# Building the routing lists per expert group by group in a graph-and-experts kernel

## What is computed

```python
x = x + einsum(segment_sum(layernorm(x)[src] * edge_weight[:, None], dst), W) + b
xf = layernorm(x)
H = gelu(xf @ W1 + b1)                        # 256 -> 1024
probs = softmax(H @ Wg + bg)                  # 8 experts
assign = argmax(probs)
y = H @ Wd[e] + bd[e]                         # for the assigned e only: 1024 -> 256
x = x + probs[assign] * y
```

## Time and profile before

| | us |
|---|---|
| median of 3 runs | 2820.1 |
| lowest and highest run | 2818.66, 2824.56 |
| span of the profiled execution | 2820.7 |
| PE busy, DVE busy, ACT busy, POOL busy in it | 2418.9, 988.5, 444.4, 1847.0 |

### The profile page before, as it was taken

How to read it: one execution, slowest core, us unless ns; L and a number is a source line. 1 busy time by engine, 2 the same in 40 slices (tenths; PEclk the granted TensorE clock), 3 DMA queues, 4 the chain that set the end, 5 groups by cost and what they waited for, 6 DMA issues and landing times.

```text
span 2820.7 us, 40486 instructions
## 1 busy us (share of the span) xinstructions
PE 2418.9 (86%) x11774; PEld 1410.7 (50%) x11775; DVE 988.5 (35%) x2788; ACT 444.4 (16%) x847; POOL 1847.0 (65%) x1988
## 2 busy tenths in 40 slices
PE   0468998998889889899899899898998968999998
PEld 0133444444444444444444444444444447888887
DVE  8421333333333323333233333233332463333332
ACT  7000011000111000110001101011100102443442
POOL 0677777777777777777777777777777103555553
PEclk9988999999999999999999999999999989999999
DMA  9433444444444444444444444444444254555553
GB/s 390 151 111 112 149 146 137 120 140 149 147 149 125 126 149 148 147 141 120 138 145 148 147 118 132 148 150 148 143 121 133 90 177 129 184 183 176 183 184 126
DMA packets 153599, 420.32 MB, mean 149 GB/s; under 512 B 33320, under 2 KB 67499, under 8 KB 150880
## 3 DMA queue, kind: packets, MB, share of 16 engines
q0 software_dynamic: 100032, 300.27, 35.8%
q1 hardware_dynamic: 53536, 119.73, 11.4%
HBM read 328.02 MB, written 92.82 MB: 149 GB/s over the span
## 4 chain that ended last, share of the span: by engine, by line
POOL 46%; PE 31%; issue 17%; DVE 2%; DMA 2%; DVEq 0%; ACT 0%; SPq 0%; POOLq 0%; ACTq 0%
POOL big L391 46%; PE psA L519 4%; PE psH L560 4%; PE psA L641 3%; PE psG L641 3%; PE psH L641 3%; PE psE L641 3%; PE psR L503 2%; PE psE L509 1%; DMA src_i<-in_srcT 1%; PE psA L581 1%; PE psA L538 1%; PE psH L631 1%; PE psE L631 1%; PE psA L631 1%
## 5 line engine op out<-in xcount | busy, mean ns | idle before, releaser
L391 POOL DMA_INDIRECT big<-xn_table,src_i x1664 | 1615.2, 971 | 581.5 <-issue 580.0
L519 PE MATMUL psA<-w,ident 128*128 128x512 f32 x1664 | 735.5, 595 | 0.0
L519 PEld LDWEIGHTS psA<-w,ident 128*128 128x128 f32 x1664 | 308.5, 190 | 347.9 <-issue 347.9
L503 PE MATMUL psR<-big,sel_narrow 128*32 128x256 f32 x3328 | 258.7, 464 | 220.9 <-DMA big<-xn_table,src_i 158.6
L454 ACT ACTIVATE hidT<-psH,b 128x512 f32<-128x512 f32 x200 | 137.4, 687 | 1651.6 <-PE psH L560 1651.6
L560 PE MATMUL psH<-xn2T,w 128*128 128x512 f32 x800 | 351.4, 592 | 0.7 <-ACT xn2T L449 0.7
L503 PEld LDWEIGHTS psR<-big,sel_narrow 128*32 128x32 f32 x3328 | 116.0, 128 | 369.0 <-issue 333.5
L877 DVE COPY parts<-psR 128x512 f32<-128x512 f32 x104 | 71.8, 690 | 563.3 <-PE psR L503 562.9
L560 PEld LDWEIGHTS psH<-xn2T,w 128*128 128x128 f32 x800 | 152.1, 190 | 181.5 <-issue 179.2
L509 PE MATMUL psE<-w,ident 128*128 128x512 f32 x416 | 224.2, 664 | 0.0
L405 POOL COPY stage<-rel_f 128x1 int32 (+1 forms) x105 | 19.2, 183 | 250.9 <-DVEq L1065 144.3
(11 more groups left out here) (203 smaller groups left out, 2343.4 us busy)
## 6 DMA issues: line engine op xcount, KB each, us to landing
row_table<-rows SPq DMA_DIRECT2D x25, 2064.0 KB, 7.9
big<-xn_table,src_i POOLq DMA_INDIRECT x1664
big<-in_x SPq DMA_DIRECT2D x10, 1280.0 KB, 17.4
xn_table<-big SPq DMA_DIRECT2D x10, 1280.0 KB, 12.8
big<-in_x SPq DMA_DIRECT2D x25, 512.0 KB
row_table<-big SPq DMA_DIRECT2D x25, 512.0 KB, 3.9
big<-in_Wd SPq DMA_DIRECT2D x8, 1024.0 KB, 11.9
hidT<-in_dstT SPq DMA_DIRECT2D x2, 840.0 KB, 30.3
```

Source lines behind the costliest of these rows:

```text
L391: nc.gpsimd.indirect_dma_start(out=xring[:, h * STEP_TILES + j, :], out_offset=None, in_=xn_dram[:, :], in_offset=bass.IndirectOffsetOnAxi ...
L503: mm = nc.tensor.matmul(psQ[j * LANES:(j + 1) * LANES, o * C:(o + 1) * C], sel_narrow[:, t, :], xring[:, t, :], start=(odd == 0), stop=(od ...
L519: nc.tensor.matmul(psA[0][:, :], ident[:, :], w1[:, 0, 0:512], start=True, stop=True)
```

## The change

It builds the order of nodes by expert while the groups are worked on, in place of behind the loop.

- `choose`, at the end of `second_part(f)`, turns group f's logits into a one-hot of its nodes' experts (`chosen`), on DVE.
- `rank_list`, at the start of `hidden(f)` on PE, ranks the choices of group f-1 within their experts: 8 matmuls. `rank_choices` on DVE, between normalisation and evictions, makes a column one-hot and four slot one-hots of them. `extend_list`, on PE behind the hidden matmuls, multiplies these: 4 matmuls. `add_to_lists` on DVE adds the result to eight lists (128 x 104 each) at places that it loads into registers, and counts.
- Behind the loop, groups 23 and 24 are still to be listed. Then DVE pads the counts, copies the eight lists one after another into `merged` at register places, each over the padding of the one before, and works out owners and node numbers as it did.
- All of the routing from L978 to L1041, L609 to L624 and the buffer `logits` go.
- SP loads `Wd` and `bd` when the last edge step and the last take of sums are through, ahead of the store of group 24's rows.
- DVE's loop has one place for a group's first part (group 0's too), `second_part` behind it under its own If, and the wide variant as a loop of two tiles with two one-hot buffers in place of four.

The core of the diff:

```diff
@@ SP
-            store_rows(NF - 1)
-            sp.wait_ge(s_main, 1)
+            sp.wait_ge(s_edge_mm, TILES + MM0)
+            sp.wait_ge(s_ffn, (NF - 1) * FFN_LINKS + 2)
             for e in range(E):
                 sp.dma_start(wd[:, e * HC:(e + 1) * HC, :],
                              Wd[e].rearrange("(c p) o -> p c o", p=P)).then_inc(s_wd, 16)
             sp.dma_start(bd_bc, bd.rearrange("e c -> (e c)").partition_broadcast(P)).then_inc(s_bd, 16)
+            store_rows(NF - 1)
@@ PE
+            def rank_list(b):
+                pe.wait_ge(s_chosen, b + 1)
+                oh = chosen[:, :, :].rearrange("p q e -> p (q e)")
+                at, total = list_rank, list_total
+                nc.tensor.matmul(psE[0][:, at], upper[:, :], oh, start=True, stop=False)
+                for d in range(1, QB):
+                    nc.tensor.matmul(psE[0][:, at.start + d * E:at.stop], ones[:, :], oh[:, 0:(QB - d) * E],
+                                     start=False, stop=(d == QB - 1))
+                for q in range(QB):
+                    mm = nc.tensor.matmul(psE[0][:, total], ones[:, :], oh[:, q * E:(q + 1) * E],
+                                          start=(q == 0), stop=(q == QB - 1))
+                mm.then_inc(s_rank, 1)
+
+            def extend_list(b):
+                pe.wait_ge(s_rank_oh, b + 1)
+                for q in range(QB):
+                    mm = nc.tensor.matmul(psE[0][:, list_new], slot_oh[:, q, :], col_oh[:, q, :],
+                                          start=(q == 0), stop=(q == QB - 1))
+                mm.then_inc(s_list, 1)
             def hidden(f, following=None):
+                rank_list(f)
                 pe.wait_ge(s_xtc, f * KC + KC)
...
                     mm.then_inc(s_h, 1)
+                extend_list(f)
                 pe.wait_ge(s_gelu, f * HC + HC)
...
                 pe.wait_ge(s_gc, f + 1)
+                pe.wait_ge(s_listed, f + 1)
@@ DVE
+            def rank_choices(tie, b):
+                dve.wait_ge(s_chosen, b + 1)
+                dve.wait_ge(s_rank, b + 1)
+                dve.sem_inc(s_pass_dve, 1)
...
+                nc.vector.tensor_tensor(col_oh[:, :, :],
+                                        iota[:, 0:LIST_COLS].unsqueeze(1).to_broadcast([P, QB, LIST_COLS]),
+                                        column.unsqueeze(2).to_broadcast([P, QB, LIST_COLS]), ALU.is_equal)
+                for q in range(QB):
+                    o = nc.vector.tensor_scalar(slot_oh[:, q, :], iota[:, 0:P], slot[:, q:q + 1],
+                                                node1[:, bass.ds(b * QB + q, 1)], ALU.is_equal, ALU.mult)
+                o.then_inc(s_rank_oh, 1)
+            def add_to_lists(tie, b):
+                dve.wait_ge(s_list, b + 1)
+                dve.sem_inc(s_pass_dve, 1)
+                full = load_columns(full_i[0:1, :], DVE, LIST_WIDTH - REACH)
+                tie(nc.vector.tensor_tensor(count[:, :], psE[0][:, list_total], count[:, :], ALU.add))
+                for e in range(E):
+                    win = lists[:, e, bass.ds(full[e], REACH)]
+                    at = list_new.start + e * REACH
+                    o = nc.vector.tensor_tensor(win, psE[0][:, at:at + REACH], win, ALU.add)
+                o.then_inc(s_listed, 1)
+                dve.wait_ge(s_listed, b + 1)
+                tie(nc.vector.tensor_copy(full_i[:, :], count[:, :]))
...
-                nc.vector.tensor_copy(logits[:, bass.ds(f * QB, QB), :], lg).then_inc(s_rows, 1)
+                dve.sem_inc(s_rows, 1)
+                choose(tie, f)
...
+                with dve.If(kind >= SECTIONS):
...
+                    take_sums(link, f, g, slot, spill)
+                    normalize(link, f)
+                with dve.If(kind == SECTIONS):
...
+                    rank_choices(tie, before)
+                    add_to_lists(tie, before)
+                    second_part(tie, before)
                 with dve.If(kind < SECTIONS):
                     gather_step(n.with_bounds(min_val=0, max_val=NG - 1))
-            second_part(NF - 1)
+            rank_choices(tie, NF - 1)
+            add_to_lists(tie, NF - 1)
+            second_part(tie, NF - 1)
+            rank_choices(tie, NF)
+            add_to_lists(tie, NF)
...
+            firsts = load_columns(first_i[0:1, :], DVE, NT)
+            for e in range(E):
+                route(nc.vector.tensor_copy(merged[:, bass.ds(firsts[e], LIST_WIDTH)], lists[:, e, :]))
```

More of the change, by code:

```diff
@@ L170, in build @@
         nmr = sb("nmr", [P, NB])
-        logits = sb("logits", [P, NB, E])
+        lists = sb("lists", [P, E, LIST_WIDTH])
+        count = sb("count", [P, E])
+        full_i = sb("full_i", [P, E], I32)
+        column0 = sb("column0", [P, E])
+        e_rank = sb("e_rank", [P, E])
+        node1 = sb("node1", [P, NB + QB])
+        valid = sb("valid", [P, NB])
+        chosen = sb("chosen", [P, QB, E])
+        route_a = sb("route_a", [P, QB, E])
+        route_b = sb("route_b", [P, QB, E])
+        route_q = sb("route_q", [P, 7, QB])
+        col_oh = sb("col_oh", [P, QB, LIST_COLS])
         perm_i = rel_f[:, 0:NT].bitcast(I32)
@@ L188, in build @@
         u = [selv[:, a * STEPS:(a + 1) * STEPS] for a in range(7)]
[L190 to L194, removed]
-        small = xn2T[:, :, :].rearrange("p a b -> p (a b)")
[L196 to L203, removed]
+        small = xn2T[:, :, :].rearrange("p a b -> p (a b)")
+        e_mod, e_pad, e_cum, e_start = (small[:, a * E:(a + 1) * E] for a in range(4))
+        first_i = small[:, 4 * E:5 * E].bitcast(I32)
+        part1 = small[:, P:P + 1]
+        tile0, owner, empty, node = (small[:, 2 * P + a * P:2 * P + a * P + NT] for a in range(4))
+        merged = gate_parts[:, 0:NT + LIST_WIDTH]
+        list_rank = slice(2 * GATE_COLS, 2 * GATE_COLS + QB * E)
+        list_total = slice(3 * GATE_COLS, 3 * GATE_COLS + E)
+        list_new = slice(4 * GATE_COLS, 4 * GATE_COLS + LIST_COLS)
         psA = [psum("psA0"), psum("psA1")]
@@ L603, in _ @@
             hidden(NF - 1)
[L606 to L624, removed]
+            rank_list(NF)
+            extend_list(NF)
             def transposes(t3, i):
@@ L933, in first_part, with second_part @@
                 o.then_inc(s_xn2, 1)
[L934 to L936 removed]
+            def second_part(tie, f):
                 dve.wait_ge(s_rows_free, f + 1)
@@ L999, in _ @@
-            route(o)
-            for e in range(E):
-                o = nc.vector.tensor_tensor_scan(incl[:, e, :], ones[:, 0:NB], total[:, e, :], 0.0,
-                                                 ALU.mult, ALU.add)
-            route(o)
+            tie = Ticker(dve, s_rt, (NF - 1) * LIST_LINKS)
+            rank_choices(tie, NF - 1)
[3 more added lines that the diff above has]
+            add_to_lists(tie, NF)
+            route = Ticker(dve, s_rt, (NF - 1) * LIST_LINKS + tie.n)
@@ L1051, in _ @@
             nc.vector.tensor_scalar(texp_i[:, :, 1], owner, float(C), None, ALU.mult)
-            dve.wait_ge(s_pm, PM0 + NB + 1)
-            node1 = psG[:, 0:NT]
-            empty, node = (where.rearrange("p e b -> p (e b)")[:, a * P:a * P + NT] for a in range(2))
-            route(nc.vector.tensor_scalar(empty, node1, 1.0, -1.0, ALU.min, ALU.mult))
+            node_of = merged[:, 0:NT]
+            route(nc.vector.tensor_scalar(empty, node_of, 1.0, -1.0, ALU.min, ALU.mult))
             route(nc.vector.tensor_scalar(empty, empty, 1.0, None, ALU.add))
-            route(nc.vector.scalar_tensor_tensor(out=node, in0=empty, scalar=part1, in1=node1,
+            route(nc.vector.scalar_tensor_tensor(out=node, in0=empty, scalar=part1, in1=node_of,
                                                  op0=ALU.mult, op1=ALU.add))
```

185 lines of the change are left out of this document (87 added, 98 removed).

## The result

The changed kernel takes 2830.9 us in the median of 4 runs (2829.8 to 2832.4), 1.0041 times the kernel before (95% interval 1.0027 to 1.0055): **slower by 0.4%**, by 10.4 us against the median beside it. The forecast was 2801.6 us and faster; the range held the result, the direction was wrong.

The account below looks back on a forecast made before the run. POOL's gathers bound the kernel, with PE 7.5 us per group step behind. Later last group step +15.5, that step +8.0, last hidden stage +3.0, tail -45.0: -18.5, 2802.2, as median 2801.6 us; range 2788 to 2857.

Parts of the forecast that it names:

- (a): Group step, PE: eight rank matmuls ahead of the hidden stage add 1.65 us.
- (b): Group step: PE waits while VectorE turns ranks into one-hots behind its normalisation, 3.1 us.
- (c): Group step, PE: four list matmuls with two hand-overs, 1.1 us.
- (d): Group step: VectorE's list additions ahead of its evictions, 3.45 us (3.1 to 4.7), in place of 2.57 before.
- the rival in which it costs per register: Loading eight registers takes 2.2 us, not 0.45; D is 9.7, the time 2846 us, slower; chance 0.04.
- (f): Group step: half clock on PE behind its wait for the one-hots, 0.85 us, between 0 and 2.5.
- (e): `choose` on VectorE delays `place` of the next step; PE waits 0.4 us on the mean, between 0 and 1.0.
- D: What the change adds to PE's time per group step: 8.0 us, between 6.3 and 10.8.
- the first rival: PE's clock and hand-overs cost more: D 9.7, 2842 us, slower; decides from D = 9.0; chance 0.23.
- a tie: Case with D between 8.55 and 9.0, moving the sum by under 5.6 us; chance 0.13.
- The last group and the tail: Last group step 8.0 us longer, last hidden stage 3.0; from last logits to routed stage 21.2 for 66.2, 45.0 less.
- At nothing: Counted as free: some 2.5 us of new constants ahead of step 0, the looped wide variant, the shared first group.

Follow-up runs that it names:

- Experiment 3: The kernel before, without lists, with 8 or 11 dummy matmuls on PE in each group step behind the gate sums: 2836.2 us and 2866.2 us.
- experiment 2: One dummy matmul less per edge step (FILL 7, not 8): changed kernel 2783.5 us, 0.9882 of the kernel before; the kernel before, same edit, 2818.8 us, 0.9998.
- experiment 1: The changed kernel with four dummy matmuls filling PE's wait for the one-hots: 2808.1 us, 0.9965 of the kernel before.
- experiment 5: The changed kernel with the one-hots moved ahead of the normalisation and FILL at 7 instead of 8: 2790.0 us, 0.9896 of the kernel before.

## Why the prediction was wrong

- **The bound, right.** PE's margin of 7.5 us per group step decided the case, and each microsecond above it costs 23. Experiment 3 shows the margin, experiment 2 that PE sets the pace above it.
- **(a) Rank matmuls, right:** 1.65 counted, 1.70 measured.
- **(b), (c), (d) together, right:** 5.1 counted; with the clock held (experiment 1) wait, list matmuls, gate sums and transposes take 3.85 + 1.01 + 1.85 + 6.15 = 12.86 us where 0.78 + 1.86 + 5.41 = 8.05 stood before: 4.8 more. The register load of eight took 0.612 us in the median where I took 0.45 (line L316, ns min/median/max), far under the 2.2 of the rival in which it costs per register:

```profile
L316 DVEq TENSOR_LOAD <-full_i x26: 599/612/1200, 302.3 to 2340.5; - x26
```

- **(f) The clock, mis-sized:** 0.85 counted, 1.63 measured, within its bounds of 0 to 2.5. I said that a part of the loss lies beside VectorE's list work; it does, but it is the smaller part: 2.29 lost, 0.66 hidden.
- **(e) `choose`, mis-sized:** 0.4 counted; the last two lines of the table by stretch have 1.13, over its bound of 1.0. Of this 0.78 is the step behind. The waits of PE for `parts` grew from 3.2 us in 8 to 30.2 in 19. Before, 11 of the 23 steps behind a group step had a part at half clock, which covered VectorE's lateness; now 4 have, and the others run at full clock and meet the late VectorE. VectorE at such a place, from the logits to `place`, the one-hots with which PE places the next step's partial sums, before and now:

```profile
1077.16 0.19 DVE L947 TENSOR_TENSOR rows<-psE,bg_bc 128x32 f32<-128x32 f32 x1
1077.65 0.18 DVE L953 COPY logits<-rows 128x32 f32 x1 [0.30 <-DVE rows L947]
1082.20 0.33 DVE L871 TENSOR_TENSOR place<-iota,shift_f 128x160 f32<-128x160 f32 x1 [4.37 <-issue]
```

```profile
1100.69 0.19 DVE L1032 TENSOR_TENSOR rows<-psE,bg_bc 128x32 f32<-128x32 f32 x1
...
1102.26 0.19 DVE L996 TENSOR_TENSOR chosen<-route_b,valid 128x32 f32<-128x32 f32 x1
1107.37 0.32 DVE L897 TENSOR_TENSOR place<-iota,shift_f 128x160 f32<-128x160 f32 x1 [4.92 <-issue]
```

In the mean of the 23, `place` comes 6.91 us behind the logits where it came 5.07. `choose` itself is 1.10 of the 1.84, near the 1.2 counted. The other 0.74 is idle time in front of `place`, in which two register loads of VectorE's sequencer lie; they take 1.78 and 1.27 us in place of 1.14 and 0.96. PE's own load ahead of its step takes 0.83 in place of 0.48: that is the 0.35 of (e) that isn't in the step behind. These loads run beside the store of rows (1101.16 to 1108.57 us in this cycle, with the DMA share at 1.00 from 1102.70 on), and VectorE's first one now starts 1.92 us behind that store's issue, not 0.62. The prediction put them at nothing. No run leaves `choose` out, so whether it is what moved them into the store is not shown.
- **The step that failed** is the sum D = 8.0: (f) and (e), some 0.75 us too small each, make the 9.36 of it. 23 x 1.36 is 31 us, and the 4 us that I added for margin that can't be used weren't needed: +41.9 in place of +15.5. D is where the first rival decides (from 9.0, chance 0.23); by its own formula 9.36 gives 2834 us. But its mechanism is only a good half of the miss: the half clock held through list matmuls and gate sums, not through the transposes, and with (f) alone put right D would be 8.8, a tie by the prediction's own bounds. It took (e) as well. For (f) the mistake was to choose a middle, since I had PE idle for 3 to 4 us and the row behind such a wait has the half clock; for (e) it was not to count that the half clock, once it falls ahead, no longer covers VectorE in the step behind, and the register loads.
- **The last group and the tail, right:** +12.3 for 11.0 and -44.1 for -45.0.
- **Wd, right** that it is hidden: bd is issued at 2328.81 and POOL is freed at 2353.01 by VectorE's own work (2352.44), without a wait for the loads. That the move is needed for it, 14.6 us, the prediction didn't say.
- **At nothing, right:** the first gather starts at 76.94 us (76.91 before), step 4 at 182.41 (182.33). The wide variant ran in no step; its loop wasn't tried.

## What to carry to other kernels

A long tail that is moved into a loop is paid once per turn, so the loop's margin per turn on the engine that must do the work is the price limit: here 7.5 us against a count of 8.0 and a measured 9.36, and 0.1 us of error in that count is 2.3 us of time. Where a hand-over makes TensorE wait, count the matmuls behind it at both clock levels (here, behind waits of 3.6 to 3.9 us, they took 2.29 us more), and look for a stretch in which the other engine idles anyway: the same work in another place turned 0.4% slower into 1.0% faster. Work that is hidden only because its neighbour is slow comes into sight when the neighbour is mended.

## What the runs showed of the hardware

In the changed kernel 24 gathers of POOL begin while VectorE adds the bias `gnn_b_bc` to a group's rows, an addition with both inputs in SBUF (L1010). Each of the 24 ends 0.81 to 0.82 us behind the end of the addition, whenever it began. POOL and VectorE at one of them:

```profile
373.58 0.95 POOL L404 DMA_INDIRECT big<-xn_table,src_i  x1 [0.30 <-issue]
374.83 1.88 POOL L404 DMA_INDIRECT big<-xn_table,src_i  x1 [0.30 <-issue]
```

```profile
374.67 1.23 DVE L1010 TENSOR_TENSOR big<-big,gnn_b_bc 128x1024 f32<-128x1024 f32 x1
```

The gather ends at 376.71, 0.81 us behind the addition's end. Its offsets (`src_i`) lie in SBUF. The Trainium skill, "SBUF — State Buffer", section "Who interferes with whom", says that a VectorE instruction with both inputs in SBUF contends with a GpSimd instruction that reads SBUF; the trace agrees, with 0.93 us more for this gather. Where gathers and additions happen to meet differs from kernel to kernel. The sum over all 1664 gathers, from the page of the changed kernel and of the changed kernel with FILL at 7:

```profile
L404 POOL DMA_INDIRECT big<-xn_table,src_i x1664 | 1616.7, 972 | 603.7 <-issue 578.3
```

```profile
L404 POOL DMA_INDIRECT big<-xn_table,src_i x1664 | 1600.0, 962 | 583.2 <-issue 580.1
```

The second has 16.7 us less. 15.2 of it lie at this one addition: the gathers that begin in it, 24 in either kernel, take 20.5 us more in sum than as many at the usual 0.946 us with FILL at 8, and 5.3 more with FILL at 7, since there they begin later in it. The last gather ends at 2185.2 us, ahead of the kernel before (2198.7), and the 16.7 us are more than the 6.5 by which experiment 2 beat its range. Whether the meetings can be steered wasn't tried; experiment 5, with the same edit in another kernel, didn't repeat it.
